# An RWKV attention layer with a 32-expert MoE on one core: z moved to ScalarE, its norm weights to the experts' split, one scan for the counts, and a new order of the rounds and seams

## The chip, the cores and the metric

One core of a Trainium2 chip. The time is the device time of one execution in microseconds. The kernel before has a median of 1735.44 us over 3 runs (1730.95 to 1735.58).

## The reference

`x` is 8 sequences of 512 tokens with 512 channels. With `xn` the layer norm of `x`, the output is `x + attention(xn) + ffn(xn)`:

```python
# attention (xx = previous token - token)
k, v, r, g = (xn + xx * tm_i) @ W_i.T        # four projections
wkv = scan over tokens: out = (a + e^u e^k v) / (b + e^u e^k); a = w a + e^k v; b = w b + e^k
o = (sigmoid(r) * wkv * sigmoid(g)) @ Wo.T ; attention = layernorm(o) * ln_g + ln_b
# ffn
z = w_norm * rmsnorm(xn)
probs = softmax(z @ w_router) ; 4 of 32 experts per token, at most 256 tokens per expert
out = sum of the 4 experts' (silu(z @ w_gate) * (z @ w_up)) @ w_down * prob
out += sigmoid(z @ w_shared_gate) * ((silu(z @ sw_gate) * (z @ sw_up)) @ sw_down)
```

Matrix products have fp32 accuracy: each operand is split into a rounded high part and the rest (`_hi`, `_lo`), and three products replace one.

## The kernel before

Everything is on one core, in three stages, each with hand-written orders of work for five queues (`sync`, `gpsimd`, `scalar`, `vector`, `tensor`). Engines meet only at semaphores; within a queue the order in the code is the order of execution, so an instruction that waits holds all that is queued behind it.

**Projection stage** (lines 115 to 1019): 8 rounds, one for each sequence. `first_round`, `one_round(1)`, a loop of two rounds, `one_round(6, tail=True)` and `last_round`. A round b holds: layer-norm statistics (`norm_stats`, `norm_scales`), `make_xn`, transposes on TensorE (`turn_xn`), the mixes for K, V, R and G (`make_mix` L681 on VectorE; `mix_hi` L455 on ScalarE; `mix_lo` L358 on GpSimd), the four projections (`project`, L957, each in two halves of 24 matmuls), exponentials, sigmoids and gates (`exp_k`, `gate_r` L470, `gate_g`, `make_ekv`, `make_gate` L702). For the FFN: z by token (`make_z` L629, VectorE), stored to HBM rows, and z transposed (`make_zT`, L650 and L657), from which `score` has the router's logits. `choose` (L705) finds the top 4, one-hot rows, and the running count `seen` (four additions, L733); `count` on TensorE turns the counts into positions; `assign` (L738 to L767) makes slots and weights; `scatter` (L372) writes token numbers into a table in HBM, 16 indirect DMAs a round issued by GpSimd, among the `mix_lo` of R and K.

**First seam**: in `last_round` the first experts' weights are loaded and split. After all scatters the table is read (`read_table`), indices are made, GpSimd gathers expert 0's rows of z, TensorE turns them.

**Expert stage** (L1021 to L1346): 32 experts of 256 slots. Per expert TensorE makes gate and up products for three chunks of the hidden units (`up_gate`, L1305), turns the next expert's rows (L1297), then the down product (L1332, 18 matmuls, chunk by chunk; each chunk waits for its `hidden_lo`). ScalarE's `rows_hi` (L1165) and VectorE's `rows_lo` (L1244) split the turned rows while the down product runs, and stand ahead of chunk 2's `hidden_hi` and `hidden_lo` (L1255).

**Output stage** (L1349 on): 8 batches, with 11 pieces of the shared expert each: `gate_up(f)` (L1930), `down(f)` (L1944), the output projection (L1961). Batch 0 also splits the shared weights piece by piece (`weight_hi`, `weight_lo`, `gate_lo`), `piece` holding one of each kind. VectorE's `fill(f)` puts the wkv recurrence (`sums` L1762 and L1764, `current`, `inverse`, `make_att`) and the sum over experts (`add_expert`) between the hidden products. **The second seam** is the last expert (`during_last`) and batch 0.

## Time and profile before

| | us |
|---|---|
| median of 3 runs | 1735.44 |
| the profiled execution | 1735.99 |
| its span | 1734.2 |
| projection rounds and first seam, to the first expert product | 468.0 |
| experts, to the first shared product | 435.0 |
| output stage | 831.2 |

TensorE is the busiest engine (1653.1 us), then VectorE (1275.4), GpSimd (885.7) and ScalarE (661.5). In the views, DVE is VectorE, ACT ScalarE, POOL GpSimd, PE TensorE's matmuls and PEld its weight loads. A timeline row has its start, its duration, the instruction, and in brackets how long its engine had stood still and what ended that.

### The profile page before, as it was taken

Reading aid. Unit: us, or ns where it says so; the run is one execution under the profiler, and the core shown is the slowest. Engines: PE = TensorE matmul, PEld = TensorE weight load, DVE = VectorE, ACT = ScalarE, POOL = GpSimd, SP = SyncE. Lnnn points to the kernel's source line nnn. Section 1 sums busy time; section 2 is a strip of 40 time slices with the busy share of each in tenths; the row PEclk is TensorE's granted clock in tenths of the full one; section 3 lists DMA queues with packets and bytes.
Section 4 is the critical chain, followed back from the end, with each engine's and each line's share of the span. In section 5 each row is a group of like instructions: output and inputs, shape, how many; then the busy total and the mean of one; then the engine's idle time right before and its main releaser. Section 6 shows DMA issues by size and latency. Waiting matters only on the chain.

```text
span 1734.2 us, 26081 instructions
## 1 busy us (share of the span) xinstructions
PE 1653.1 (95%) x8496; PEld 1402.8 (81%) x8496; DVE 1275.4 (74%) x1836; ACT 661.5 (38%) x1093; POOL 885.7 (51%) x733
## 2 busy tenths in 40 slices
PE   5889999998899999999998899999999999999998
PEld 4667777876699999999996688888788888888887
DVE  6999989998455555555559887786787768687776
ACT  4545545453466665666653312121121212112121
POOL 3778878886644444444436645252443524253351
PEclk9999999999999999999999999999999999999999
DMA  4354332433476666666687655465444344433431
GB/s 159 146 194 147 132 136 99 168 146 147 153 256 222 230 241 245 241 228 222 239 273 225 212 204 182 144 203 173 146 155 162 113 144 142 135 121 110 164 104 43
DMA packets 123087, 299.47 MB, mean 173 GB/s; under 512 B 20524, under 2 KB 31788, under 8 KB 118384
## 3 DMA queue, kind: packets, MB, share of 16 engines
q1 hardware_dynamic: 103248, 264.08, 42.9%
q0 software_dynamic: 19456, 33.67, 6.9%
q8 instruction: 50, 0.82, 0.2%
q10 hardware_dynamic: 288, 0.52, 0.1%
q14 instruction: 45, 0.37, 0.1%
HBM read 233.61 MB, written 81.36 MB: 182 GB/s over the span
## 4 chain that ended last, share of the span: by engine, by line
PE 69%; DVE 14%; issue 8%; POOL 4%; DMA 3%; ACT 2%; DVEq 0%; SPq 0%; POOLq 0%; ACTq 0%
PE bank L1930 24%; PE bank L1305 16%; PE bank L1944 12%; PE bank L1332 8%; PE bank L1961 5%; DVE mixf L681 3%; POOL slot_tokens L372 2%; PE bank L1297 2%; PE bank L957 2%; DMA z_rows<-z 1%; POOL mix L358 1%; DVE bank L650 1%; DVE z L629 1%; DVE s_wg L1834 1%; DVE ekv L697 1%
## 5 line engine op out<-in xcount | busy, mean ns | idle before, releaser
L957 PE MATMUL bank<-mix,w 128*128 128x512 f32 x1536 | 369.4, 398 | 27.5 <-DVE sr L702 11.0
L957 PEld LDWEIGHTS bank<-mix,w 128*128 128x128 f32 x1536 | 289.3, 191 | 97.9 <-DVE sr L702 10.6
L1930 PE MATMUL bank<-s_zT,s_wu 128*128 128x512 f32 x1056 | 256.3, 392 | 13.5 <-DVE s_act_g L1739 11.5
L1930 PE MATMUL bank<-s_zT,s_wg 128*128 128x512 f32 x1056 | 254.2, 389 | 0.7 <-ACT s_act_g L1650 0.5
L1944 PE MATMUL bank<-s_wd,s_h 128*128 128x512 f32 x1056 | 253.9, 389 | 0.9 <-DVE s_h L1745 0.9
L1930 PEld LDWEIGHTS bank<-s_zT,s_wu 128*128 128x128 f32 x1056 | 198.7, 189 | 57.9 <-issue 16.8
L1930 PEld LDWEIGHTS bank<-s_zT,s_wg 128*128 128x128 f32 x1056 | 197.9, 188 | 43.1 <-issue 1.5
L1944 PEld LDWEIGHTS bank<-s_wd,s_h 128*128 128x128 f32 x1056 | 198.1, 188 | 42.6 <-issue 1.3
L1126 POOL TENSOR_TENSOR e_wg<-e_g_in,e_wg 128x1408 fp32r<-128x1408 f32 x31 | 100.3, 3236 | 210.4 <-ACT e_wg L1150 210.4
L1562 POOL DMA_INDIRECT s_picked<-y_rows,s_slot x128 | 140.5, 1098 | 84.9 <-DVE s_total L1795 45.2
L358 POOL TENSOR_TENSOR mix<-mixf,mix 128x512 fp32r<-128x512 f32 x116 | 154.8, 1353 | 51.5 <-ACT mix L455 50.5
L1661 ACT ACTIVATE s_h<-s_act_g 128x512 fp32r<-128x512 f32 x88 | 55.6, 632 | 295.6 <-DVE s_act_g L1739 293.8
L372 POOL DMA_INDIRECT slot_tokens<-token,slot x128 | 140.8, 1100 | 47.5 <-issue 35.0
L1650 ACT ACTIVATE s_act_g<-bank 128x512 f32<-128x512 f32 x88 | 52.4, 596 | 280.8 <-PE bank L1930 274.2
L1305 PE MATMUL bank<-e_xT,e_wg 128*128 128x256 f32 (+1 forms) x1152 | 152.2, 282 | 0.0
L1305 PE MATMUL bank<-e_xT,e_wu 128*128 128x256 f32 (+1 forms) x1152 | 152.1, 282 | 0.0
L1305 PEld LDWEIGHTS bank<-e_xT,e_wg 128*128 128x128 f32 (+1 forms) x1152 | 144.3, 180 | 3.0 <-DVE e_xT L1244 0.4
L1305 PEld LDWEIGHTS bank<-e_xT,e_wu 128*128 128x128 f32 (+1 forms) x1152 | 142.1, 180 | 0.0
L1332 PE MATMUL bank<-e_wd,e_h 128*128 128x512 f32 (+1 forms) x576 | 140.1, 396 | 0.0
L1795 DVE SCALAR_TENSOR_TENSOR s_total<-s_picked,s_rec,s_total 128x512 f32<-128x512 f32 x128 | 130.2, 1017 | 3.7 <-DVE s_total L1795 0.5
L455 ACT ACTIVATE mix<-mixf 128x512 fp32r<-128x512 f32 x128 | 78.7, 630 | 131.5 <-DVE mixf L681 115.9
L1582 POOL TENSOR_TENSOR s_att<-s_gate,s_att 128x512 fp32r<-128x512 f32 x32 | 47.3, 1478 | 155.3 <-ACT s_att L1676 155.3
(158 smaller groups left out, 2451.9 us busy)
## 6 DMA issues: line engine op xcount, KB each, us to landing
s_wu<-wu_split SPq DMA_DIRECT2D x77, 512.0 KB
e_g_in<-in_w_gate SPq DMA_DIRECT2D x32, 704.0 KB
e_u_in<-in_w_up SPq DMA_DIRECT2D x32, 704.0 KB
e_d_in<-in_w_down SPq DMA_DIRECT2D x32, 512.0 KB
y_rows<-e_y SPq DMA_DIRECT2D x32, 512.0 KB, 2.9
s_zT<-zT_parts SPq DMA_DIRECT2D x16, 1024.0 KB, 7.0
zT_parts<-zT_hi SPq DMA_DIRECT2D x8, 1024.0 KB
zT_parts<-zT_lo SPq DMA_DIRECT2D x8, 1024.0 KB
```

Of the source, the lines that this page charges most:

```text
L358: pool.tensor_tensor(mix[:, i % 2, k, 1, :], mixf[:, k, :], mix[:, i % 2, k, 0, :].bitcast(F32), ALU.subtract).then_inc(lo_made, 1)
L372: pool.indirect_dma_start(d["slots"], bass.IndirectOffsetOnAxis(ap=slot[:, at:at + 1], axis=0), token[:, at // TOPK:at // TOPK + 1], None, ...
L455: act.activation(mix[:, i % 2, k, 0, :], mixf[:, k, :], ACT.Copy).then_inc(hi_made, 1)
L957: last = pe.matmul(pj[m][:], w[i][:, w_part, k, m * P:(m + 1) * P], mix[:, i % 2, k, x_part, :], start=(k == 0 and q == 0), stop=(k == KC ...
L1126: pool.tensor_tensor(wg[half][:, 1, :], g_in[half][:], wg[half][:, 0, :].bitcast(F32), ALU.subtract).then_inc(wg_lo, 1)
L1305: last = pe.matmul(gu[f][0:m, which, :], w[half][:, w_part, k * F + f0:k * F + f0 + m], xT[half][:, x_part, k, :], start=(q == 0 and k == ...
L1332: last = pe.matmul(yp[c][:], h[0:m, f, h_part, c * P:(c + 1) * P], wd[half][0:m, w_part, f, :], start=(f == 0 and q == 0), stop=(f == NF - ...
L1562: pool.indirect_dma_start(picked[:, k, :], None, d["y_flat"], bass.IndirectOffsetOnAxis(ap=slot[:, j * TOPK + k:j * TOPK + k + 1], axis=0) ...
L1795: dve.scalar_tensor_tensor(total[:, j, :], picked[:, k, :], rec[:, at:at + 1], total[:, j, :], ALU.mult, ALU.add).then_inc(picked_used, 1)
L1930: last = pe.matmul(into[:], w[:, w_part, k, :], zT[:, x_part, k, :], start=(q == 0 and k == 0), stop=(q == 2 and k == KC - 1))
L1944: last = pe.matmul(yp[j][:], h[:, i, h_part, j * P:(j + 1) * P], wd[f][:, w_part, :], start=(f == 0 and q == 0), stop=(f == NFS - 1 and q ...
L1961: last = pe.matmul(ob[j % 2][:], att[m][:, x_part, j * P:(j + 1) * P], wo[m][:, w_part, :], start=(m == 0 and q == 0), stop=(m == KC - 1 a ...
```

## The change

What it does:

- `make_z` goes to ScalarE, as xn times its rms factor, without the norm weights; z gets four buffers. The weights come in when an expert's turned rows are split: `rows_hi` and `rows_lo` work on four pieces of 256 columns with a per-partition factor. The copies of scales, slots and weights into `keep` are ScalarE's as well (`keep_route`).
- The four additions of `seen` become one `tensor_tensor_scan` over 32 x 5 columns.
- The low part of the V mix is made by VectorE, not GpSimd. The scatters of a round are spread among the low parts of R, G and K (`MORE` is 6), 4 alone at a round's start; slots and tokens have two buffers.
- `count` comes between R's halves, `assign` after G's mixes; the first gates of a round stand within `make_zT`; assign(0) moves into round 1.
- A new order for the last round: `score(LAST)` is its first product, `choose` and `assign` follow V's mixes, R's and G's low parts are VectorE's; first weights wait for V's first half, second weights' up and down parts for the gather.
- At the second seam gate pieces 1 to 4 have a buffer of their own and are split in the last expert, at four places of each queue, with the first scans, the first reciprocal and the four bases. Hidden products of the shared expert (all but the last piece) are written to PSUM.

```diff
+        def one_round(b, half, uses, second=False, tail=False):
+            last = NT * TOPK
+            if second:
+                pool.wait_ge(table_zeroed, 16)
+            at = 0 if second else MORE
+            scatter(b - 1, 1 - half, at, at + KC)
             norm_scales(b + 1, 1 - half)
-            mix_lo_among(b, R_, b - 1, MORE)
-            scatter(b - 1, MORE + KC, NT * TOPK)
-            mix_lo(b, G_)
-            scatter(b, 0, SOME)
-            mix_lo_among(b + 1, K_, b, SOME)
-            scatter(b, SOME + KC, MORE)
+            mix_lo_among(b, R_, b - 1, 1 - half, at + KC, last)
+            if second:
+                scatter(b - 1, 1 - half, at + 2 * KC, last - KC)
+                at = last - 3 * KC
+            mix_lo_among(b, G_, b - 1, 1 - half, at + 2 * KC, last)
+            scatter(b, half, 0, MORE - KC)
+            mix_lo_among(b + 1, K_, b, half, MORE - KC, MORE)
+            if tail:
+                scatter(b, half, MORE, last)
...
+        def make_z(b, half):
+
+            act.wait_ge(pow_step, (b + 1) * POWS)
+            for j in range(NT):
+                act.wait_ge(xn_made, b * NT + j + 1)
+                wait(act, z_stored[j], b * 16)
+                act.activation(z[:, j, :], xn[:, j, :], ACT.Copy, scale=r2[:, half, j:j + 1]).then_inc(z_made, 1)
+            act.activation(keep["rec"][:, bass.ds(b * REC, 2 * NT)], scales[:, half, :], ACT.Copy).then_inc(scales_kept, 1)
+
+        def keep_route(b, half):
+            act.wait_ge(rec_made, b + 1)
+            act.activation(keep["slot"][:, bass.ds(b * NT * TOPK, NT * TOPK)], slot[:, half, :], ACT.Copy)
+            act.activation(keep["rec"][:, bass.ds(b * REC + 2 * NT, REC - 2 * NT)], rec[:],
+                           ACT.Copy).then_inc(route_kept, 1)
...
+            if second:
+                keep_route(0, 0)
+            make_z(b + 1, 1 - half)
+            keep_route(b, half)
             gate_r(b, 0)
...
-                route.step(dve.tensor_reduce(chosen[:], oh[:].rearrange("p (j k) e -> p j e k", j=NT), AX.X, ALU.add))
+                route.link(dve.tensor_reduce(counted[:, :, 1:NT + 1], oh[:].rearrange("p (j k) e -> p e j k", j=NT),
+                                             AX.X, ALU.add))
+                dve.tensor_tensor_scan(seen[:].rearrange("p e j -> p (e j)"), fresh[:].rearrange("p e j -> p (e j)"),
+                                       counted[:].rearrange("p e j -> p (e j)"), 0.0, ALU.mult,
+                                       ALU.add).then_inc(chosen_made, 1)
             dve.tensor_scalar(token_id, token_id, float(T), None, ALU.add)
-            route.link(dve.tensor_copy(seen[:, 0, :], seen[:, NT, :]))
-            for j in range(NT):
-                ins = dve.tensor_tensor(seen[:, j + 1, :], seen[:, j, :], chosen[:, j, :], ALU.add)
-                if j < NT - 1:
-                    route.link(ins)
-            ins.then_inc(chosen_made, 1)
...
+        def one_round(b, half, uses, second=False, tail=False):
+            gates(b - 1, 2)
+            if second:
+                assign(0, 0, 0)
             for k in range(KC):
                 make_mix(b, half, V_, k)
+            for k in range(KC):
+                mix_lo(b, V_, k)
             norm_stats(b + 1)
-            if second:
-                for j in range(NT):
-                    make_z(1, 1, j)
             for k in range(KC):
                 make_mix(b, half, R_, k)
             choose(b)
-            make_z(b + 1, 1 - half, 0)
-            make_z(b + 1, 1 - half, 1)
-            make_ekv(b, 0)
-            make_ekv(b, 1)
-            make_z(b + 1, 1 - half, 2)
-            make_z(b + 1, 1 - half, 3)
-            keep_scales(b + 1, 1 - half)
-            make_mix(b, half, G_, 0)
-            make_mix(b, half, G_, 1)
-            make_ekv(b, 2)
-            make_ekv(b, 3)
-            make_mix(b, half, G_, 2)
-            make_mix(b, half, G_, 3)
-            assign(b)
+            for m in range(KC):
+                make_ekv(b, m)
+            for k in range(KC):
+                make_mix(b, half, G_, k)
+            assign(b, half, uses)
             for k in range(KC):
                 shift_difference(b + 1, 1 - half, k)
-            if tail:
-                make_zT(LAST, FIRST_HALF)
             for k in range(KC):
                 make_mix(b + 1, 1 - half, K_, k)
-            if not tail:
-                make_zT(b + 1, 1 - half)
-            make_gate(b, 0)
-            make_gate(b, 1)
+            make_zT(b + 1, 1 - half, lambda: gates(b, 0))
...
         def last_round():
+            gates(LAST - 1, 2)
+            for k in range(KC):
+                make_mix(LAST, FIRST_HALF, V_, k)
             choose(LAST)
+            for k in range(KC):
+                mix_lo(LAST, V_, k)
+            assign(LAST, FIRST_HALF, B // 2 - 1)
+            for k in range(KC):
+                make_mix(LAST, FIRST_HALF, R_, k)
+            for k in range(KC):
+                mix_lo(LAST, R_, k)
+            for m in range(KC):
+                make_ekv(LAST, m)
             for k in range(KC):
                 make_mix(LAST, FIRST_HALF, G_, k)
             for k in range(KC):
                 mix_lo(LAST, G_, k)
             first_weights()
+            gates(LAST, 0)
...
-            count(b)
             turn_xn(b + 1, 2)
             turn_xn(b + 1, 3)
             turn_r2(b + 1, 1 - half)
             project(b, R_, 0)
+            count(b)
             project(b, R_, 1)
             project(b, G_, 0)
-            if tail:
-                score(LAST)
-            project(b, G_, 1, {3: lambda: turn_score(LAST)} if tail else {})
+            project(b, G_, 1)
 
         def last_round():
-            project(LAST, K_, 0)
-            project(LAST, K_, 1, {1: lambda: count(LAST)})
+            score(LAST)
+            project(LAST, K_, 0, {2: lambda: turn_score(LAST)})
+            project(LAST, K_, 1, {3: lambda: count(LAST)})
...
+            sp.wait_ge(shared["v_done"], B * KC - 2)
             load(0, 0)
 
         def second_weights():
             sp.wait_ge(shared["r_done"], B * KC)
-            load(1, 1)
+            load(1, 1, lambda part: sp.wait_ge(gathered[0], 32))
 
         def read_table():
-            sp.wait_ge(shared["scattered"], 16 * B * NT * TOPK)
+            for half in range(2):
+                sp.wait_ge(shared["scattered"][half], 16 * (B // 2) * NT * TOPK)
             sp.dma_start(table[:], d["table"]).then_inc(table_loaded, 16)
...
         def rows_hi(e, half):
             act.wait_ge(turned, e + 1)
-            for i in range(2):
-                act.activation(xT[half][:, 0, 2 * i:2 * i + 2, :],
-                               xt[i][:].rearrange("p (k s) -> p k s", k=2), ACT.Copy).then_inc(x_hi, 1)
+            for k in range(KC):
+                turned_k = xt[k // 2][:, (k % 2) * CAP:(k % 2 + 1) * CAP]
+                act.activation(xT[half][:, 0, k, :], turned_k, ACT.Copy, scale=norm_col[:, k:k + 1]).then_inc(x_hi, 1)
...
         def rows_lo(e, half):
-            for i in range(2):
-                dve.wait_ge(x_hi, e * 2 + i + 1)
-                dve.tensor_tensor(xT[half][:, 1, 2 * i:2 * i + 2, :], xt[i][:].rearrange("p (k s) -> p k s", k=2),
-                                  xT[half][:, 0, 2 * i:2 * i + 2, :].bitcast(F32), ALU.subtract).then_inc(x_lo, 1)
+            for k in range(KC):
+                dve.wait_ge(x_hi, e * KC + k // 2 * 2 + 2)
+                turned_k = xt[k // 2][:, (k % 2) * CAP:(k % 2 + 1) * CAP]
+                dve.scalar_tensor_tensor(xT[half][:, 1, k, :], turned_k, norm_col[:, k:k + 1],
+                                         xT[half][:, 0, k, :].bitcast(F32), ALU.mult, ALU.subtract).then_inc(x_lo, 1)
...
+    def hidden_at(f, i):
+
+        return ob[f % 2][:] if f < NFS - 1 else act_g[:, i, :]
...
             weight_lo(D, 1)
+            weight_lo(D, 2)
+            pool.wait_ge(piece_lo[G], AHEAD + 1)
             pool.memset(picked[:], 0.0).then_inc(setup, 1)
+            pool.wait_ge(c_loaded, 32)
+            for j in range(NT):
...
+        def last_second():
+            weight_hi(G, 1)
+            weight_hi(G, 2)
+            weight_hi(G, 3)
+
+        def last_third():
+            weight_hi(G, 4)
+
+        def last_fourth():
+            weight_hi(U, 1)
+            weight_hi(D, 1)
+            for j in range(NT):
+                make_base(0, j)
...
             hidden_lo(e, 1)
             hidden(e, 2)
             if more:
                 rows_lo(e + 1, 1 - half)
+            else:
+                output_early[2]()
             hidden_lo(e, 2)
             if more:
                 down_lo(e + 1, 1 - half)
+            else:
+                output_early[3]()
 
...
+        def last_third():
+            gate_lo(2)
             dve.wait_ge(setup, 3)
             sums(0, 0, 0)
-            hidden(0, 0, 0)
-            rounds(dve, one_round)
-
-        return lambda: gate_lo(0), main
+
+        def last_fourth():
+            gate_lo(3)
+            gate_lo(4)
+            current(0, 0)
+            inverse(0, 0)
```

## Rows read from the trace of the kernel before

**Rows 1.** The page's first part: busy time, share of the span, instructions
```profile
PE 1653.1 (95%) x8496; PEld 1402.8 (81%) x8496; DVE 1275.4 (74%) x1836; ACT 661.5 (38%) x1093; POOL 885.7 (51%) x733
```

**Rows 2.** Busy time by stage: span, busy us (instructions) by engine, granted clock, DMA share, GB/s
```profile
79.00:141.92 62.92, 51.58 (x228) 41.10 (x227) 59.52 (x109) 30.28 (x53) 51.34 (x47) 0.95 0.36 134
...
352.37:468.04 115.67, 101.07 (x440) 80.92 (x440) 86.69 (x173) 49.38 (x80) 79.55 (x74) 0.94 0.40 148
468.00:904.00 436.00, 435.99 (x3134) 411.69 (x3134) 239.57 (x383) 269.26 (x448) 196.80 (x96) 1.00 0.67 239
903.04:1007.33 104.29, 91.56 (x386) 72.46 (x385) 92.00 (x76) 37.49 (x66) 63.99 (x49) 0.98 0.69 216
1020.93:1107.97 87.04, 87.04 (x385) 72.10 (x385) 67.42 (x69) 18.89 (x30) 36.42 (x28) 1.00 0.54 174
```

**Rows 3.** TensorE's timeline, 340 to 355 us: start, us, instruction [idle before, releaser]
```profile
343.88 6.07 PE L957 MATMUL bank<-mix,w 128*128 128x512 f32 x24 [0.25 <-ACT sr L470]
352.37 5.71 PE L957 MATMUL bank<-mix,w 128*128 128x512 f32 x24 [2.42 <-DVE sr L702]
```

**Rows 4.** Busy time, one steady projection round
```profile
300.42:352.37 51.95, 49.24 (x226) 39.57 (x227) 48.33 (x93) 26.33 (x47) 43.70 (x41) 1.00 0.38 142
```

**Rows 5.** VectorE's groups by form, 0 to 460 us: count, busy us, mean ns, idle before
```profile
L681 DVE SCALAR_TENSOR_TENSOR mixf<-xx,keep_const,xnT 128x512 f32<-128x512 f32 x128 | 124.2, 1024 | 2.7 <-POOL mix L358 2.5
L629 DVE SCALAR_TENSOR_TENSOR z<-xn,r,norm_w 128x512 f32<-128x512 f32 x32 | 35.7, 1149 | 10.3 <-DMA z_rows<-z 8.2 <-issue 1.6
L650 DVE SCALAR_TENSOR_TENSOR bank<-xnT,keep_const,bank 128x512 f32<-128x512 f32 x32 | 23.3, 750 | 0.6
```

**Rows 6.** Timeline of VectorE and GpSimd, 250 to 260 us
```profile
252.84 4.64 DVE L681 SCALAR_TENSOR_TENSOR mixf<-xx,keep_const,xnT 128x512 f32<-128x512 f32 x1
...
253.12 3.80 POOL L358 TENSOR_TENSOR mix<-mixf,mix 128x512 fp32r<-128x512 f32 x3
```

**Rows 7.** VectorE's timeline, `assign` of round 1
```profile
124.67 0.67 DVE L745 TENSOR_TENSOR oh<-oh,bank 128x512 f32<-128x512 f32 x1
...
128.74 0.21 DVE L764 TENSOR_TENSOR rec<-rec,valid 128x16 f32<-128x16 f32 x1
```

**Rows 8.** Timeline of one expert, 700 to 715 us
```profile
709.38 1.09 ACT L1165 ACTIVATE e_xT<-bank 128x512 fp32r<-128x512 f32 x2 [0.50 <-PE bank L1297]
710.01 1.29 DVE L1244 TENSOR_TENSOR e_xT<-bank,e_xT 128x512 fp32r<-128x512 f32 x2 [0.68 <-ACT e_xT L1165]
...
711.22 0.41 DVE L1255 TENSOR_TENSOR e_h<-e_act_g,e_h 96x256 fp32r<-96x256 f32 x1
711.71 0.19 PEld L1332 LDWEIGHTS bank<-e_wd,e_h 96*128 96x128 f32 x1
```

**Rows 9.** Line 1762, one of the two scans: duration ns min/median/max
```profile
L1762 DVE TENSOR_TENSOR_SCAN s_b_sum<-keep_decay,s_ek x32: 1211/1220/2326, 905.0 to 1690.5; 128x512 f32<-128x512 f32 x32
```

**Rows 10.** ScalarE's groups by form, 0 to 460 us
```profile
L455 ACT ACTIVATE mix<-mixf 128x512 fp32r<-128x512 f32 x128 | 78.7, 630 | 131.5 <-DVE mixf L681 115.9 <-issue 14.4
L428 ACT ACTIVATE xn<-x_in,scales 128x512 f32<-128x512 f32 x32 | 24.3, 806 | 37.8 <-POOL var_eps L348 21.5 <-POOL scales L347 12.5 <-DVE z L629 3.8
...
L470 ACT ACT_TABLE_LOAD x8 | 10.3, 1283 | 0.4 <-issue 0.3
```

**Rows 11.** TensorE's timeline, round 0: the first G product
```profile
67.58 11.48 PE L957 MATMUL bank<-mix,w 128*128 128x512 f32 x48 [1.42 <-issue]
```

**Rows 12.** Timeline, the first seam
```profile
426.31 0.16 DVE L755 TENSOR_TENSOR slot<-s,s 128x16 uint32<-128x16 f32 x1
...
434.23 0.98 POOL L372 DMA_INDIRECT slot_tokens<-token,slot  x1 [5.94 <-issue]
...
454.22 0.97 POOL L372 DMA_INDIRECT slot_tokens<-token,slot  x1 [0.30 <-issue]
...
464.05 1.98 PE L1297 MATMUL bank<-keep_const,e_rows 128*128 128x128 f32 x8 [8.16 <-DMA e_rows<-z_rows,keep_index]
```

**Rows 13.** TensorE's weight loads, the last expert's down product
```profile
898.78 3.99 PEld L1332 LDWEIGHTS bank<-e_wd,e_h 128*128 128x128 f32 x18
```

More of the change, by code:

```diff
@@ L365, in weight_lo, with scatter @@
                                    ALU.subtract).then_inc(w_lo[i], 1)
-        def scatter(b, first, last):
+        def scatter(b, half, first, last):
             if first == 0:
@@ L1074, in sync, with load @@
     def sync(sp):
-        def load(e, half):
+        def load(e, half, paced=lambda part: None):
             wait(sp, wg_lo, e - 1)
@@ L1197, in one_expert @@
             silu(e, 1)
+            if not more:
+                output_early[1]()
             hidden_hi(e, 1)
@@ L1267, in one_expert @@
             hidden(e, 1)
+            if not more:
+                output_early[1]()
             hidden_lo(e, 1)
```

333 lines of the change are left out of this document (160 added, 173 removed).

## The prediction

> **What bounds the kernel now.** The page's first part says TensorE is busy 95% of the span [rows 1], which leaves at most some 80 us, so the question is only where TensorE stands still. I read the busy table by stage next [rows 2]. From 468 to 904 us (experts), and in the shared expert's second batch, TensorE has no gap: there nothing can be won, only lost. The gaps are in the first 468 us (eight projection rounds), and in the first shared-expert batch, whose way from its first product to its first output projection takes 104.29 us, where the same way in the next batch takes 87.04. So at most 17.2 us lie there.
>
> Then the projection round. Four steady rounds lie between 141.92 and 352.37 [rows 2, 3], 52.6 us each; in the last of them (51.95) VectorE is busy 48.33 [rows 4]. There TensorE waits 2.42 for VectorE's gate product, 0.25 for ScalarE's sigmoid, and 24 matmuls that otherwise take 5.5 take 6.07 [rows 3]: without these a round is **48.6 us**, TensorE's floor. VectorE sets the rest, and not by its arithmetic alone: L650, which reads and writes PSUM, has a mean of 0.750 us, L681, the same operation on SBUF alone, 1.024 over 128 of them, so 35 us in all are waiting inside this one form [rows 5]. z (L629), of the same form, has a mean of 1.149. The timeline shows why: one L681 takes 4.64 and ends only after three GpSimd subtractions in a row have ended [rows 6].
> The Trainium skill, "SBUF — State Buffer", section "SBUF: two separate sides", calls this an exclusive lock: a VectorE instruction with two SBUF inputs against a GpSimd one that reads SBUF, the loser blocked entirely. The trace agrees, with 4.64 against 0.750.
>
> **Part 1, the steady projection round.** Off VectorE go: four z (4 x 1.15 = 4.6, and waits for z's stores), the copies of scales, slots and weights (about 0.8), four count additions and a copy (bounds 0.9, at 0.17 to 0.21 as `assign`'s short steps [rows 7], and 2.1 if they are stretched too; 1.6 taken), and the one long wait of [rows 6], since no four subtractions in a row are left on GpSimd (about 3.9). On it come: four V subtractions (0.69 each as L1244 [rows 8], 2.8), one scan of 160 columns (bounds 0.4 and 0.8, by 512 columns at 1.2 or 2.3 [rows 9]; I take 0.6) and a copy (0.17). Net 10.9 - 3.6, about -7: VectorE falls from 48.3 to some 41, under the floor. GpSimd loses 4 x 1.35 and keeps 16 scatters; ScalarE takes z at 4 x 0.8 as L428 [rows 10] and the copies, 26.3 of 52 us [rows 4] become 30. z and the copies there are hidden behind matmuls as long as ScalarE is ahead of its sigmoids.
> That is the catch. The position count moves from after V to between the halves of R, and ScalarE's copy of the route (it waits for the end of `assign`) is queued ahead of gate_r(b,0). Counted from the end of R's first half: count 0.15, `assign` from L745 to L764 4.28 with one stretched step [rows 7] and one copy more, 4.4; two short copies 0.45 (as two or three of `assign`'s short steps); the table load 1.28 [rows 10] and a sigmoid of 0.6: 6.9 us. TensorE comes to G after 5.5 and needs it: it waits 1.4 (bounds 0.5 if nothing in `assign` is stretched, 3 if two steps are). So a round is 48.6 + 1.4 = 50.0, and the wait for VectorE's gates goes, since gates(b,0) now stand ahead of most of make_zT. Rounds 2 to 5: 4 x (52.6 - 50.0) = **-10.4**.
>
> **Part 2, the first rounds.** In round 0 G starts at 67.58 after a wait of 1.42 [rows 11]. Without z, choose(0) starts some 5 us earlier; G then starts with the end of R's second half and the transposes, at 65.4, 2.2 sooner, and the count (0.3) is later: **-2.5**. ScalarE's z(0), 2.9 us, delays the G weights, but GpSimd is busy until later. Round 1 takes 62.92 with TensorE busy 51.58 [rows 2]: 11.3 of waits, for the count (late by the stretched additions) and for K, where GpSimd's scatters stand between the subtractions. The count moves to a place where it isn't late, the scatters go out of K. But assign(0) comes in (4.2 on VectorE), norm_scales follow 2 to 3 us later, and transposes wait 0.7: 48.6 + 1.4 + 0.7 = 50.7 (the granted clock of 0.95 in that row taken as full again without the waits), **-12.2**.
>
> **Part 3, the last two rounds and the first seam**, 115.67 us [rows 2]. Now: the slots of the last round are ready at 426.3, then 16 scatters run to 455.2, of which 5.94 is one hold of the queue; the gather lands at 464.05 after TensorE stood 8.16 [rows 12], and the first expert product is at 468.04. After: round 6 is 50.0, score(LAST) waits 0.8 for zT. From its start: slots at 15 (logits 4.8, choose 5.2, V subtractions 2.6, half of assign 2.4); GpSimd has by then put out round 6's ten scatters (10 x 1.27 = 12.7; one is 0.97 + 0.30 [rows 12]). Sixteen are 20.3, and from the last one to the landed gather 8.9 pass as now: 44.2 without a hold, 50.1 with one. TensorE is there at 44.5. I take half, 3, and 4.2 from turn to product as now: 50.0 + 0.8 + 44.5 + 3 + 4.2 = 102.5, **-13.2** (bounds -16 and -8; the weight loads now start after V's first half and so fall among these scatters, as they do now around the hold). Sum of parts 1 to 3: **-38** (bounds -44 and -22).
>
> **Part 4, the experts, where I expect a loss.** The norm weight goes into the split of the turned rows: 2 ScalarE copies of 512 columns become 4 of 256 with a pointer scale, 2 VectorE subtractions become 4 scalar_tensor_tensor. Behind them on VectorE stands the subtraction for the third hidden chunk, which TensorE's down product needs at its weight load of 711.71. Today it ends at 711.22 + 0.41 = 711.63 [rows 8]: 0.08 us of cover. Now: two ScalarE copies take 1.09, so one per 0.49; 256 columns 0.30 to 0.35 each. A pointer scale and bias cost 0.17 in duration and 0.05 in spacing (L428 0.806 against L455 0.630 [rows 10]). Two of 256 are there at about 710.1 to 710.3 instead of 710.01. VectorE: two subtractions take 1.29, one per 0.60; a scalar_tensor_tensor takes 0.06 more than such a subtraction for 512 (L650 0.750 [rows 5] against 0.69), so 0.39 for 256: 4 x 0.39 = 1.56 against 1.20. Late by 0.12 to 0.30 + 0.36, less the cover: 0.4 to 0.6 per expert. I take 0.5: 31 x 0.5 = **+15.5** (bounds: +6 if only the extra starts count, +39 by the rival below). The down product has no other slack, as TensorE is never idle here.
> The Trainium skill, "ScalarE: Activation LUTs", section "Rules for kernel authors", budgets about 0.3 us per ACTIVATE with a pointer bias and 0.83 ns per element. By it, as an estimate, four of 256 are 2.05 us against 1.45 for two of 512, and if they don't overlap the third chunk is 1.0 late: +31 us in place of +15.5. The two copies of [rows 8] take 1.09 where the budget has 1.45, so I stay with the sum.
>
> **Part 5, the second seam**, 17.2 us at most. Gate pieces 1 to 4, the first scans, the bases and one reciprocal move into the last expert, and the hidden product goes to PSUM, which takes VectorE's waits for the port away from its subtractions. But in the last expert both scans stand ahead of the third chunk's subtraction: gate_lo 0.7 and two scans of 1.2 to 2.3 each [rows 9], 3.1 to 5.3 in all. The third chunk is made at 899.94; with these and its own subtraction of 0.4 it is split at 903.4 to 905.6. The down product starts its loads at 898.78 [rows 13] and wants it after 12 of them, 2.6 later, at 901.4: 2.0 to 4.2 lost, 3.5 taken, since GpSimd is busy beside. GpSimd then has in a row the wait for D2 (silu(0) + 0.6), its 1.3, the memset 1.8, four base additions 5.2 and four gathers 5.2 (each as a scatter, 1.27) ahead of U2's split: TensorE waits some 2.4. With 2.5 left of today's waits (12.7 by the busy table [rows 2]): 8.4 of 17.2 remain, **-9** (bounds -13 and -2). The other seven batches: all changes are off TensorE's path and VectorE has slack; 0, bounds -1 and +2.
>
> **Sum.** Span 1734.2; 1734.2 - 38 + 15.5 - 9 = 1702.7. The profiled run reports 1735.99, 1.8 above its span, and the median is 1735.44: **1704 us**.
>
> **Rivals.** (a) The third chunk isn't late: were ScalarE's pieces and VectorE's to overlap better than the spacings, the cover holds. For it: ScalarE's copies from PSUM overlap already (1.09 for two of 0.6). Against: 0.08 us of cover. 1704 - 15 = 1689. (b) The route copy blocks more: `assign` is stretched in two or three steps beside alternating scatters and subtractions, and the sigmoids and K's copies behind it are late as well; 2.5 us more in seven rounds, 1721. For it: its waits in [rows 7]; against: it has one such step today. (c) The scaled copies don't overlap at all: 0.41 + 0.17 = 0.58 each, the fourth at 711.70, the third chunk at 712.92, 1.25 late, 39 us for 15.5: 1728. The skill's budget, in the sentence above, lies between this and the forecast. (d) **Slower**: each scaled copy holds ScalarE as long as L428 does for 512 columns, 0.80: four take 3.2 in place of 1.0, the third chunk is 2.1 late, 65 us in the experts: 1754. It decides from 47 / 31 = 1.5 us per expert on. Against it: half the columns. (e) VectorE isn't relieved in the rounds because its waits move to other instructions: rounds stay at 52.6 and parts 2 and 3 bring half, 1727.
>
> **How the numbers follow.** Forecast 0.47, (a) 0.17, (b) 0.16, (c) 0.09, (d) 0.04, (e) 0.07. The forecast's own range is 1694 to 1714; with (a), (b) and most of (c) the range is 1685 to 1727, which leaves out 2 in 10. About 0.3% (5 us) is what a measurement of this kernel can tell from no change. Faster by more: all but (d) and the high ends of (c) and (e): 0.92; same 0.03; slower 0.05.
>
> **What would show it.** In the profile after: rounds at 50 us with a wait of the G product for ScalarE's sigmoid, none for VectorE's gates; no L681 over 2 us in V; VectorE near 41 per round; first expert product at 430. An expert period of 14.1 instead of 13.62 with a TensorE wait in the down product; no wait there means (a), over 15 means (d). In the second seam one wait of 3 to 4 us in the last expert's down product and one for U2's split. Wrong would be: a new hold of a queue in the last round, or z on ScalarE late for xn.

## The result, and the profile after

The changed kernel takes 1738.14 us (median of 9 runs), the kernel before 1734.13 us beside it: a ratio of 1.0027, 95% interval 1.0016 to 1.0039. The prediction was 1704 us, with 1685 to 1727 as its range. The profiled execution has a span of 1736.3 us, against 1734.2.

The sum hides two shifts that cancel. In the table each stage ends where TensorE starts the next one's first product.

| stage | before | after | difference | predicted |
|---|---|---|---|---|
| start to the first expert product | 468.04 | 454.99 | -13.0 | -38 |
| experts, to the first output product | 435.0 | 451.76 | +16.8 | +19 (15.5 and 3.5) |
| first output batch, to its first attention product | 104.3 | 101.2 | -3.1 | -12.5 |
| the rest | | | +1.5 | 0 |

The page of the kernel after, first part (compare [rows 1]), and its busy table (columns as in [rows 2]; the rows are the first output batch, the next one, one steady projection round, and the stretch of [rows 4]):

```profile
PE 1662.9 (96%) x8496; PEld 1405.3 (81%) x8496; DVE 1243.6 (72%) x1848; ACT 693.3 (40%) x1213; POOL 848.5 (49%) x707
```
```profile
906.75:1007.91 101.16, 90.60 (x385) 72.66 (x384) 82.03 (x72) 32.88 (x58) 62.52 (x48) 0.98 0.65 209
1021.51:1108.55 87.04, 87.04 (x385) 72.07 (x384) 67.56 (x69) 18.53 (x30) 36.39 (x28) 1.00 0.54 173
281.06:334.25 53.19, 50.37 (x226) 40.94 (x227) 41.33 (x87) 29.13 (x53) 37.05 (x36) 0.96 0.38 138
300.42:352.37 51.95, 49.13 (x223) 40.23 (x222) 40.46 (x86) 28.14 (x52) 38.03 (x36) 0.97 0.37 135
```

VectorE's busy time in a round fell from 48.3 us to 41.3, as predicted, ScalarE's went to 29 and GpSimd's to 37. No engine beside TensorE is near the round's length, and the round still takes 53.0 us (mean of rounds 2 to 5) against 52.6. TensorE's timeline, every wait for the first product of G (start, us, instruction, idle before and releaser):

```profile
122.08 18.21 PE L934 MATMUL bank<-mix,w 128*128 128x512 f32 x72 [4.19 <-ACT sr L486]
176.05 18.19 PE L934 MATMUL bank<-mix,w 128*128 128x512 f32 x72 [3.60 <-ACT sr L486]
229.25 16.60 PE L934 MATMUL bank<-mix,w 128*128 128x512 f32 x72 [2.82 <-ACT sr L486]
281.06 18.18 PE L934 MATMUL bank<-mix,w 128*128 128x512 f32 x72 [3.03 <-ACT sr L486]
334.25 17.93 PE L934 MATMUL bank<-mix,w 128*128 128x512 f32 x72 [2.82 <-ACT sr L486]
387.14 12.77 PE L934 MATMUL bank<-mix,w 128*128 128x512 f32 x48 [2.77 <-ACT sr L486]
438.18 11.40 PE L934 MATMUL bank<-mix,w 128*128 128x512 f32 x42 [2.70 <-ACT sr L486]
```

The wait for VectorE's gates (2.42 in [rows 3]) has turned into a wait for ScalarE's sigmoid: the place that the prediction named, at twice its size or more. A second cost follows some of these waits, and not all. 72 matmuls take 18.2 us at 122.08, 176.05 and 281.06 and 17.9 at 334.25; at full clock they take 16.6 (72 x 0.23), and so they do at 229.25. The granted clock is 0.62 of full speed from 334.3 to 338.0, right after the wait, so most of that stretch runs at the lower of its two levels, 1.2 GHz; from 229.25 to 233.0, after a wait of the same 2.82 us, it is 1.00.

What ScalarE waited for stands on VectorE and GpSimd, in the round of 334.25:

```profile
326.06 0.69 DVE L748 TENSOR_TENSOR oh<-oh,bank 128x512 f32<-128x512 f32 x1 [2.86 <-PE bank L912]
326.78 2.43 DVE L750 COPY counted<-seen 128x32 bf16<-128x32 bf16 x1
329.09 0.67 DVE L751 TENSOR_REDUCE pos<-oh 128x16 f32<-128x512 f32 x1
...
331.53 0.22 DVE L769 TENSOR_TENSOR rec<-rec,valid 128x16 f32<-128x16 f32 x1
```
```profile
326.57 2.56 POOL L354 TENSOR_TENSOR mix<-mixf,mix 128x512 fp32r<-128x512 f32 x2
```
```profile
331.87 0.22 ACT L450 ACTIVATE keep_slot<-slot 128x16 uint32 x1 [5.46 <-DVE rec L769]
332.00 0.20 ACT L451 ACTIVATE keep_rec<-rec 128x20 f32 x1
332.22 1.28 ACT L486 ACT_TABLE_LOAD   x1
333.51 1.09 ACT L486 ACTIVATE sr<-bank 128x512 f32<-128x512 f32 x2
```

R's first half has been done since 325.5, yet ScalarE is idle for 5.46 us, because its copy of the route stands ahead of the sigmoids and waits for VectorE's last step. A copy of 32 columns takes 2.43 us in that chain, next to two GpSimd subtractions in a row; alone, in the last round, it takes 0.21. Of the rounds with a longer wait, the one of 176.05 has this copy at 3.00. The one of 122.08 has it at 0.27, and there two later steps of 16 columns are the long ones:

```profile
114.87 2.01 DVE L760 TENSOR_TENSOR slot<-s,s 128x16 uint32<-128x16 f32 x1
...
117.42 1.92 DVE L766 TENSOR_TENSOR rec<-ex,rtot 128x16 f32<-128x16 f32 x1
```

In the experts the third chunk's subtraction ends later than in [rows 8], and TensorE waits a little in every down product (TensorE and VectorE, expert at 700 us):

```profile
707.54 1.67 PE L1327 MATMUL bank<-e_wd,e_h 96*128 96x512 f32 x6 [0.20 <-DVE e_h L1244]
```
```profile
705.50 1.66 DVE L1233 SCALAR_TENSOR_TENSOR e_xT<-bank,keep_const,e_xT 128x256 fp32r<-128x256 f32 x4 [0.92 <-ACT e_xT L1148]
707.08 0.41 DVE L1244 TENSOR_TENSOR e_h<-e_act_g,e_h 96x256 fp32r<-96x256 f32 x1
```

The expert period is 14.11 us instead of 13.62. The row shows 0.20 us of waiting, but the wait costs more: the 18 products of the down projection take 4.70 us from their start to the next gate product, and 4.22 in the run below where the wait is gone.

### The profile page after: what moved, and what is told of

It is laid out like the page before. It is cut to its first block, busy times and chain, and to the rows that moved or that the text cites. A ratio compares the mean times of both kernels' runs of the same rounds, so it can differ in the third digit from the quotient of the medians.

```text
span 1736.3 us, 26220 instructions
## 1 busy us (share of the span) xinstructions
PE 1662.9 (96%) x8496; PEld 1405.3 (81%) x8496; DVE 1243.6 (72%) x1848; ACT 693.3 (40%) x1213; POOL 848.5 (49%) x707
## 4 chain that ended last, share of the span: by engine, by line
PE 75%; DVE 11%; issue 5%; ACT 3%; POOL 3%; DMA 2%; DVEq 0%; ACTq 0%; SPq 0%; another core or an unknown queue 0%; POOLq 0%
PE bank L1986 23%; PE bank L1300 15%; PE bank L934 13%; PE bank L2000 12%; PE bank L2017 5%; PE bank L1327 3%; DVE e_xT L1233 2%; PE bank L1292 2%; ACT e_xT L1148 2%; POOL slot_tokens L368 1%; PE bank L876 1%; PE bank L893 1%; DVE mixf L686 1%; DVE e_h L1244 1%; DVE s_total L1838 1%
## 5 line engine op out<-in xcount | busy, mean ns | idle before, releaser
L934 PE MATMUL bank<-mix,w 128*128 128x512 f32 x1536 | 375.3, 403 | 26.9 <-ACT sr L486 21.9
L934 PEld LDWEIGHTS bank<-mix,w 128*128 128x128 f32 x1536 | 295.6, 195 | 93.9 <-issue 26.0
L1108 POOL TENSOR_TENSOR e_wg<-e_g_in,e_wg 128x1408 fp32r<-128x1408 f32 x31 | 101.2, 3263 | 223.4 <-ACT e_wg L1132 223.4
L1327 PE MATMUL bank<-e_wd,e_h 128*128 128x512 f32 (+1 forms) x576 | 149.1, 403 | 7.7 <-DVE e_h L1244 7.7
L1686 ACT ACTIVATE s_h<-bank 128x512 fp32r<-128x512 f32 x80 | 47.8, 598 | 265.7 <-DVE bank L1782 265.7
L354 POOL TENSOR_TENSOR mix<-mixf,mix 128x512 fp32r<-128x512 f32 x88 | 120.4, 1378 | 47.0 <-ACT mix L471 45.9
L1838 DVE SCALAR_TENSOR_TENSOR s_total<-s_picked,s_rec,s_total 128x512 f32<-128x512 f32 x128 | 138.3, 1080 | 3.7 <-DVE s_total L1838 0.5
L1327 PEld LDWEIGHTS bank<-e_wd,e_h 128*128 128x128 f32 (+1 forms) x576 | 103.6, 189 | 40.7 <-DVE e_h L1244 21.2
```

The lines of the kernel that those rows point to most:

```text
L354: pool.tensor_tensor(mix[:, i % 2, k, 1, :], mixf[:, k, :], mix[:, i % 2, k, 0, :].bitcast(F32), ALU.subtract).then_inc(lo_made, 1)
L934: last = pe.matmul(pj[m][:], w[i][:, w_part, k, m * P:(m + 1) * P], mix[:, i % 2, k, x_part, :], start=(k == 0 and q == 0), stop=(k == KC ...
L1108: pool.tensor_tensor(wg[half][:, 1, :], g_in[half][:], wg[half][:, 0, :].bitcast(F32), ALU.subtract).then_inc(wg_lo, 1)
L1327: last = pe.matmul(yp[c][:], h[0:m, f, h_part, c * P:(c + 1) * P], wd[half][0:m, w_part, f, :], start=(f == 0 and q == 0), stop=(f == NF - ...
L1838: dve.scalar_tensor_tensor(total[:, j, :], picked[:, k, :], rec[:, at:at + 1], total[:, j, :], ALU.mult, ALU.add).then_inc(picked_used, 1)
```

## The experiments

Each run is compared with the kernel before on the same chip. To compare it with the changed kernel I divide its ratio by 1.0027 and take 1738 us as 1. The ratios given in the expectations of the first four runs were meant against the changed kernel.

| run | median us | ratio to before, 95% | against the changed kernel |
|---|---|---|---|
| e1_route_late | 1722.7 | 0.9939 (0.9923 to 0.9956) | -15 |
| e2_copy_late | 1729.4 | 0.9975 (0.9965 to 0.9984) | -9 |
| e3_chunk_first | 1722.6 | 0.9938 (0.9919 to 0.9957) | -15 |
| e4_no_weights | 1721.2 | 0.9936 (0.9919 to 0.9954) | -16 |
| e5_second_seam | 1737.6 | 1.0030 (1.0018 to 1.0042) | +1 |
| e6_all | 1706.3 | 0.9840 (0.9824 to 0.9857) | -32 |
| e7_v_on_gpsimd | 1744.5 | 1.0068 (1.0051 to 1.0085) | +7 |
| e9_gate_first | 1706.8 | 0.9843 (0.9825 to 0.9861) | -32 |
| e10_z_on_vector | 1725.2 | 0.9954 (0.9936 to 0.9971) | -13 |
| e11_no_seam | 1706.9 | 0.9837 (0.9821 to 0.9854) | -33 |

**The route copies behind the sigmoids.**

```diff
@@ scalar, one_round
-            keep_route(b, half)
             gate_r(b, 0)
 ...
             gate_r(b, 3)
+            keep_route(b, half)
@@ scalar, last_round
+            for m in range(KC):
+                gate_r(LAST, m)
             first_gate_up()
             keep_route(LAST, FIRST_HALF)
-            for m in range(KC):
-                gate_r(LAST, m)
```

> In every projection round after the first, ScalarE's copies of the route (keep_route of the round's own batch) go behind the four sigmoids of R (behind gate_r(b, 3)), and in the last round the four sigmoids also go ahead of the first expert's weight copies; nothing else changes. Theory A (the 3 us wait of TensorE for the first sigmoid of R is the wait of ScalarE for VectorE's route, and the slow restart of TensorE after it is part of its price): the wait for sr in rounds 1 to 6, 21.9 us in 7, falls under 4 us, the 18.2 us of the following 72 matmuls fall back to 16.6, rounds go from 53.0 to 49 to 50 us, the first expert product moves from 454.99 to about 432, and the kernel is 20 to 25 us faster (ratio 0.986 to 0.989). Theory B (the sum of VectorE's work and the contention with GpSimd fixes the round): the wait moves to another operand and rounds stay within 1 us of 53.0, ratio 0.996 to 1.002.

The wait for the sigmoid is gone from every round. Rounds 2 to 5 take 48.9 to 49.5 us, at a granted clock of 1.00. That is theory A, and 3.8 us a round for the position of two short copies, slow matmuls behind the wait included. VectorE's sum does not bound the round: it is busy 44.4 of 49.3 us here and nobody waits for it. The total came out smaller than expected (15 us, not 20 to 25; first expert product at 440.06, not 432), because the last round has a limit of its own. TensorE's timeline of this run:

```profile
382.29 1.14 PE L893 MATMUL bank<-zT_lo,wr 128*68 128x512 f32 x4 [2.48 <-DVE zT_lo L661]
...
435.46 1.98 PE L1292 MATMUL bank<-keep_const,e_rows 128*128 128x128 f32 x8 [6.12 <-DMA e_rows<-z_rows,keep_index]
```

score(LAST) starts 17.8 us sooner (382.29 against 400.07), but the 16 scatters on GpSimd follow the slots, most of them 1.27 us apart, and the gather now ends the wait: 6.12 us, where the changed kernel, being late, waited 1.56.

**The copy of the counts behind the route.**

```diff
@@ vector, assign
             dve.wait_ge(pos_read, b + 1)
-            dve.tensor_copy(counted[:, :, 0], seen[:, :, NT])
 ...
             dve.tensor_tensor(weight, weight, valid[:], ALU.mult).then_inc(rec_made, 1)
+            dve.tensor_copy(counted[:, :, 0], seen[:, :, NT])
```

> VectorE's copy of the counts into the scan's input (the 32 columns counted <- seen in assign), which took 2.43 us beside GpSimd's low parts, goes to the end of assign, behind the last step of the route; it can then stretch nothing that ScalarE waits for. Theory A (the stretched copy is what made the chain from R's first half to the route 8.75 us instead of the 6.9 predicted): the route is ready about 2 us earlier in rounds 1 to 5, TensorE's wait for the first sigmoid falls from about 2.9 to about 1 us, each round gets 2 to 3.5 us shorter (with the half-clock restart), the kernel 10 to 17 us faster (ratio 0.990 to 0.994). Theory B (it is the port that is held and not this copy: whichever small operation of VectorE comes next then waits in its place): the chain keeps its length and the kernel is within 3 us of the changed one (0.998 to 1.002).

Between the two theories. VectorE in the same round (compare L750 above):

```profile
322.31 0.69 DVE L748 TENSOR_TENSOR oh<-oh,bank 128x512 f32<-128x512 f32 x1 [2.86 <-PE bank L912]
323.03 0.69 DVE L750 TENSOR_REDUCE pos<-oh 128x16 f32<-128x512 f32 x1
323.75 1.67 DVE L751 TENSOR_SCALAR valid<-pos 128x16 f32<-128x16 f32 x1
...
326.97 0.22 DVE L768 TENSOR_TENSOR rec<-rec,valid 128x16 f32<-128x16 f32 x1
```

The reduction passes unhindered, and the next small step, a tensor_scalar of 16 columns, takes 1.67 instead of 0.17. The hold has moved, and 0.8 us of it is gone. The Trainium skill, "SBUF — State Buffer", section "SBUF: two separate sides", has copies and tensor_scalar in two-port modes fully blocked while a GpSimd instruction holds the shared pair; the trace agrees, with 2.43 for the copy and 1.67 for the tensor_scalar, each until GpSimd's second subtraction has ended.
In rounds 2 to 5 the waits for the sigmoid are 2.68, 2.01, 2.23 and 2.01 us; in the changed kernel they are 3.60, 2.82, 3.03 and 2.82. So 0.8 to 0.9 us is gone from each. Rounds 2 and 3 got shorter by just that (53.97 to 53.03 and 51.60 to 50.81 us). Rounds 4 and 5 gained 2.1 to 2.4 us (53.39 to 50.99 and 52.94 to 50.80), since TensorE also restarts at full clock:

```profile
278.91 16.59 PE L934 MATMUL bank<-mix,w 128*128 128x512 f32 x72 [2.23 <-ACT sr L486]
329.69 16.60 PE L934 MATMUL bank<-mix,w 128*128 128x512 f32 x72 [2.01 <-ACT sr L486]
```

Of the 6.3 us that four rounds gained, 3.3 are wait and 2.9 are clock. That the shorter wait brought the clock back is not shown: a wait of 2.82 us is followed by 16.60 in one round of the changed kernel and by 17.93 in another, and in two of the runs below, which leave the rounds as they are, by these (the first e3_chunk_first, the second e4_no_weights):

```profile
229.76 19.43 PE L934 MATMUL bank<-mix,w 128*128 128x512 f32 x72 [2.82 <-ACT sr L486]
335.36 16.59 PE L934 MATMUL bank<-mix,w 128*128 128x512 f32 x72 [2.82 <-ACT sr L486]
```

**The third chunk ahead of the next rows, and the rows without the weights.** The first moves hidden_hi(e, 2) ahead of rows_hi(e + 1) on ScalarE and hidden_lo(e, 2) ahead of rows_lo(e + 1) on VectorE:

```diff
             hidden(e, 2)
+            if not more:
+                output_early[2]()
+            hidden_lo(e, 2)
             if more:
                 rows_lo(e + 1, 1 - half)
-            else:
-                output_early[2]()
-            hidden_lo(e, 2)
```

> In the experts the two halves of the third hidden chunk (hidden_hi(e, 2) on ScalarE, hidden_lo(e, 2) on VectorE) go ahead of the copies and differences of the next expert's turned rows; the number of instructions is unchanged. Theory A (the experts' 0.49 us each are the third chunk standing behind four instructions instead of two): TensorE's wait for e_h in the down product disappears, the period falls from 14.11 to 13.62, minus 15 us (ratio 0.990 to 0.992). Theory B (the longer rows' work itself is the price): the wait moves to the next expert's rows or to the down product's weights, of which down_lo now ends later, and the period stays above 14.0 (ratio 0.998 to 1.002).

> The norm weights are left out of the experts: the turned rows are copied and subtracted in two instructions of 512 columns on each engine, as before the change, without the per-partition factors (this leaves the weights out of the experts' input). All else is the changed kernel. Theory A (the four scaled copies and four scaled differences in the place of two and two cost the experts' 0.49 us): the period falls from 14.11 to 13.6, minus 15 to 16 us (ratio 0.990 to 0.992). Theory B (the period was lengthened by something else of the change, such as the early loads of the output stage): it stays at 14.1 (ratio 0.999 to 1.001).

The stage of the experts took 451.76 us in the changed kernel, 437.1 in the first run and 436.4 in the second. Theory A in both: the four scaled pieces are the cause, and the price is the third chunk's place behind them, not their work. In the reordered run all pieces are there, TensorE's wait in the down product is gone (but for 1.34 us in the last expert, whose order is unchanged), and nothing else is late:

```profile
701.54 4.38 PE L1327 MATMUL bank<-e_wd,e_h 128*128 128x512 f32 x18
```

(In the first run's profile the stage ahead, which it doesn't touch, took 5 us longer than in the changed kernel's, at a granted clock of 0.95 instead of 0.97; the medians show the experts' 15 us.)

**The second seam.** GpSimd's weight_lo(U, 2) goes ahead of the first gathers, and VectorE's sums(0, 0, 0) from ahead of hidden_lo(e, 2) to behind it.

> Two moves in the seam from the experts to the output stage, the rest is the changed kernel: GpSimd splits the shared expert's up piece 2 (weight_lo(U, 2)) ahead of the first four gathers instead of behind them, and VectorE's first two scans of the last expert (sums(0, 0, 0)) go behind the subtraction of the third hidden chunk. Theory A (the order on GpSimd and on VectorE is the price in this seam): TensorE's wait of 3.55 us for s_wu at 926.79 and the slow 12 matmuls behind it (4.61 instead of 2.9) go, 5 us, and the wait of 1.35 us in the last down product goes; from the first product of the output stage to the first attention product the time falls from 101.2 to 96 us, the kernel is 5 to 7 us faster than the changed one. Theory B (VectorE's sum of work in the first batch, whose waits of 0.6 to 1.8 us in seven chunks follow later, sets this stage): what is gained at the front comes back as longer waits for VectorE's hidden products, and the stage stays above 99 us, gain 1 to 3 us.

Both waits went and nothing was gained: theory B, though not for its reason. The stage of the experts is 2.0 us shorter, the first output batch 4.2 longer (105.4). TensorE in that batch:

```profile
920.18 4.41 PE L1987 MATMUL bank<-s_zT,s_wg 128*128 128x512 f32 x12 [2.94 <-ACT s_act_g L1676]
...
932.72 4.58 PE L1987 MATMUL bank<-s_zT,s_wg 128*128 128x512 f32 x12 [2.70 <-ACT s_act_g L1676]
```

ScalarE was itself waiting, for a piece of weights and then for VectorE's attention product, in the same run:

```profile
918.16 0.63 ACT L1726 ACTIVATE s_wg<-s_piece 128x512 fp32r<-128x512 f32 x1 [5.75 <-DMA s_piece<-in_sw_gate]
...
931.46 0.63 ACT L1705 ACTIVATE s_att<-s_gate 128x512 fp32r<-128x512 f32 x1 [5.67 <-DVE s_gate L1829]
```

SP issues that piece behind the load of down piece 2, which waits for GpSimd to split piece 1. Both waits end at about the same moment of the kernel as in the changed one (its two copies start at 916.95 and 930.53), though the batch began 3.4 us sooner. So the start of the batch moved, and what it waits for did not.

**All moves together**, with one more: VectorE's two index copies go between gate_lo(0, 0) and up_lo(0, 0) in first_weights.

> All the moves together: the route copies behind the sigmoids in the rounds and the last round, VectorE's copy of the counts behind the route, the third hidden chunk ahead of the next rows, the two moves of the second seam, and in the last round VectorE's two index copies between the differences of the first gate and up weights instead of behind both (GpSimd's first gather waited 1.6 us longer for them in the run with the route copies moved). If the gains add: 15.4 + 15.6 + 5 to 7 + 1.5 us below the changed kernel's 1738, so 1698 to 1701, the ratio to the kernel before 0.979 to 0.981, with rounds of 49.2 us, an expert period of 13.6 and the first expert product at 438. If they share a cause or VectorE becomes the bound of the rounds, less than 30 us come out, 1708 or more.

32 us below the changed kernel and 28 below the kernel before: the best of all kernels here, with two others equal to it. The moves of rounds and experts add (rounds of 49.0, experts 435.6 us, first expert product at 437.90). What misses the 1698 to 1701 is the first output batch, 104.8 us. GpSimd's split of U1 next to VectorE's moved scans:

```profile
872.63 4.57 POOL L1620 TENSOR_TENSOR s_wu<-s_piece,s_wu 128x512 fp32r<-128x512 f32 x1 [4.40 <-ACT s_wu L1726]
```

In the changed kernel it takes 2.79. The second seam's run, the only other one with the scans moved, has 4.29 there, and a batch of 105.4 us.

**The scans back, the first gated product ahead of the gathers.**

> The run with all moves, but with VectorE's scans of the last expert left where the change has them (ahead of the third chunk's subtraction), and with GpSimd's first gated product (gated_sum(0, 0)) also ahead of the first gathers. In the run with all moves the stage from the first product of the output stage to the first attention product took 104.8 us, against 101.2 in the changed kernel, although TensorE's waits for U2 and for the third chunk were gone. Theory A (the late scans ran beside GpSimd's split of U1, which took 4.57 us instead of about 2.2, so the load of down piece 2 and, behind it on SP's queue, every later piece came 2 us late, and ScalarE's sigmoid products stood behind VectorE's first attention product, which waits for GpSimd behind the gathers): the stage falls to 96 to 99 us, the kernel to 1698 to 1702, ratio to the kernel before 0.979 to 0.982, with the 1.35 us wait of the last down product back. Theory B (the pieces' DMAs themselves are late in this seam, whatever the order): the stage stays at 101 us or more, 1703 to 1707.

The numbers are those of theory B: the batch takes 101.9 us. The split of U1 takes 2.30 us again and 2.9 us of the 104.8 are gone, but not the 6 to 9 of theory A. The split of down piece 3 stands behind the gathers, as it does in the changed kernel, and with it the load of piece 4. ScalarE in this run:

```profile
902.91 0.63 ACT L1727 ACTIVATE s_wd<-s_piece 128x512 fp32r<-128x512 f32 x1 [7.48 <-DMA s_piece<-in_sw_down]
```

**Without the two seam moves.**

> The run with all moves, without the two moves in the seam to the output stage (U2's split stays behind the gathers, the scans ahead of the third chunk's subtraction): route copies late, copy of the counts late, third chunk first, index copies between. The two seam moves together gained nothing by themselves (1737.6 against 1738.1 us of the changed kernel). Theory A (moves in different stages add): the stage from the first output product to the first attention product is back at 101 us and the kernel at 1703 to 1707, that is within 3 us of the run with all moves (1706.3). Theory B (an earlier start of the output stage makes its piece loads later against TensorE, so the seam takes back part of what the rounds and experts give): more than 1708.

Theory A: 100.7 us for the batch, and the same total within the intervals. In the profiles of the other runs that leave this seam as the change has it, the batch takes 100.9 to 102.4 us (101.2 in the changed kernel), so 100.7 and 101.9 can't be told apart. Outside that scatter lie only the two kernels with the scans moved, 104.8 and 105.4. Moving U2's split together with the gated product is worth nothing that these runs can show; U2's split without the scans' move was not run alone.

**Two parts of the change undone**, each in the kernel with the route copies late.

> The run with the route copies moved (rounds of 49.2 us) with one part of the change undone: the low parts of V's mixes in rounds 1 to 6 are made by GpSimd again, as in the kernel before, and not by VectorE. Theory A (moving them bought something, since GpSimd with its scatters was the later engine): TensorE waits for mix_lo of V or R behind GpSimd's scatters, rounds grow to 50 to 52 us, the kernel is 5 to 15 us slower than that run (ratio to the kernel before 0.997 to 1.002). Theory B (TensorE hides either): rounds stay within 0.3 us of 49.2 and the ratio stays at 0.994; then this part of the change bought nothing by itself.

> The run with the route copies moved (rounds of 49.2 us), with another part of the change undone: from round 1 on VectorE makes z again (four products of 512 columns by the row scale, without the norm weights, which stay with the experts), between its route and its products of V, and ScalarE only copies the scales. Theory A (taking z from VectorE was needed): VectorE's 41 us per round become 44 to 45, and with the waits for V, R and the route TensorE waits again: rounds of 50 to 52 us, 5 to 15 us slower than that run (ratio to the kernel before 0.997 to 1.003). Theory B (VectorE had room for it): rounds stay within 0.4 us of 49.2, ratio 0.993 to 0.995.

V's low parts back on GpSimd cost 22 us: rounds 2 to 5 go from 49.2 to 52.3 us in the mean, with waits in three of them each for xn (1.6 to 1.7, behind GpSimd's scales) and for the sigmoid (1.4 to 1.6). Theory A, beyond its range. z back on VectorE gives rounds of 49.5, 49.2, 52.0 and 49.2 us (50.0 in the mean; the long one has waits of 0.80 for xn and 1.82 for the sigmoid), VectorE is busy 47.8 of 50 us, and the kernel takes 1725.2 against 1722.7 us. The intervals overlap, so of z no more is shown than that it is worth little once V and the route are settled.

## Why the prediction was wrong

Point by point, in its own steps.

**The floor of a round and VectorE's relief (part 1): right.** 48.6 us was predicted for a round without waits (51.95 less its three terms is 48.7), and the run with the route copies late has 48.9 to 49.5. VectorE went to 41.3, 41 predicted. Rival (e) is out as a mechanism, though rounds did stay at 53: VectorE was relieved, and another wait took the place.

**The wait for gate_r (part 1): the step that failed.** The place, the releaser and the queue position were right, the size was not. The chain from the end of R's first half to TensorE's restart takes 8.75 us (325.50 to 334.25) and was put at 6.9. `assign` takes 5.69 instead of 4.4, because its copy of 32 columns is held for 2.43, and 0.5 passes before it starts. This is rival (b) in kind, with one held step in rounds 2 to 5 and two in round 1. The waits of rounds 2 to 5 are therefore 3.60, 2.82, 3.03 and 2.82, 3.1 in the mean, instead of 1.4.

The sum then put at nothing what such a wait can cost behind it. In three of the four rounds the next 72 matmuls took 1.3 to 1.6 us more than at full clock, 1.1 a round in the mean. So the 3.0 us between the predicted 50.0 and the 53.0 measured are 1.7 of wait, 1.1 of clock and 0.2 of floor: 12 us in rounds 2 to 5, of which 6.7 are wait and 4.5 clock. The rows that would have warned are in the kernel before, where one of two like waits is followed by slow matmuls (granted clock 0.77 from 193.62 to 201, and 1.00 from 246.72 to 252.5):

```profile
193.62 7.34 PE L957 MATMUL bank<-mix,w 128*128 128x512 f32 x24 [2.34 <-DVE sr L702]
246.72 5.77 PE L957 MATMUL bank<-mix,w 128*128 128x512 f32 x24 [2.32 <-DVE sr L702]
```

The 6.07 of [rows 3], which the prediction took away as 0.57 too long, is not such a case: it stands ahead of the wait of 2.42, at a granted clock of 1.00.

**The first rounds (part 2): half right.** K of round 1 starts at 75.9 as predicted (76.5), but round 1 then waits 2.34 for the score and 4.19 for the sigmoid, each with 1.5 to 1.6 us of half clock behind it, and takes 58.7 us from score to score for 50.7 forecast.

**The last rounds and the first seam (part 3): too good.** No long hold came (2.27 behind the first scatter, 5.94 before), where the sum took half of one. But the last round has the same fault as the others: keep_route(LAST) stands behind the first expert's weight copies and ahead of the sigmoids, another 2.70. The run without it shows what was mis-sized beside: the score waits 2.48 for zT (0.8 forecast) and the gather 6.12 (3 forecast), 4.8 us of the 10 between the predicted 430 and its 440.06; GpSimd's subtractions in round 1, five waits of 0.5 to 1.1 between its scatters, are 4.4 more. The gather is late because each term of its chain was too small: the first scatter starts 19.8 us after the score (15 for the slots in the sum), the sixteen take 22.9 (20.3), and 10.5 pass from the last to the turn of the gathered rows (8.9).

**The experts (part 4): right.** 0.49 us each against 0.5 predicted, with the mechanism shown by two runs. Of the two parts of the term, ScalarE's four pieces take 1.57, for 1.2 to 1.4 by the 0.30 to 0.35 each of the sum, and VectorE's four 1.66, predicted 1.56. The Trainium skill, "ScalarE: Activation LUTs", section "Rules for kernel authors", would give an estimated 2.05 for ScalarE's four; the trace has 1.57. Rivals (a), (c) and (d) are out. (In (c), 712.92 is 1.21 us behind 711.71, not 1.25, which makes 1726 of its 1728.) The wait in the last down product was 1.35, not 3.5, as the scans were not stretched (1.2 each).

**The second seam (part 5): mis-sized.** U2's split is late as predicted (3.55 against 2.4), with half clock behind it (4.61 us for 12 matmuls that take 2.9, granted clock 0.60), and 7.0 us of waits for VectorE's hidden products are left where 2.5 were forecast. The batch gained 3.1 us where 12.5 were in the sum. In the experiments, taking the wait for U2 away left the batch no shorter; what sets the 14 us above the next batch's 87.04 stays open.

The signs: of the forecast's 34 us of error, 12 are the route wait and its clock in four rounds, 13 the other rounds and the first seam, 9 the second seam; the experts came out 2 us better and the later batches 1.5 worse. The chance of 0.92 for faster rested on parts 1 to 3, whose bounds (-44 to -22) did not hold -13. Both ends were worked out at full clock, while TensorE's busy time for the same matmuls up to the first expert product is 408.7 us, as it was before (407.7), and 403.5 in the run with the route copies late.

## What to carry to other kernels

A short copy that nobody needs soon is dangerous on an in-order queue when it waits for the end of another engine's chain: cost each instruction queued behind it, not the copy. A wait that a change creates costs its length and, sometimes, slow matmuls after it. Read both off all the waits of that length that the trace already has, and put the second into the bounds: here it came after some and not after others. When work is inserted ahead of something that has only 0.08 us of cover, try the order the other way round first: here the order gave back all of the 15 us.

## What was not expected of the hardware

- The length of a wait of TensorE doesn't tell what follows it. After 2.82 us the next 72 matmuls took 16.6, 17.9 and 19.4 us in different rounds and runs. After 2.0 to 2.2 they took 16.6 in rounds 3 to 5 of the run with the copy late, but after 2.13 in its round 1 the granted clock was 0.61 for 4 us. What decides is not shown.
- The smallest instructions are held as long as large ones: L750, 32 columns of bf16, takes 0.213 at its shortest, 2.428 in the median and 2.995 at its longest over the eight rounds (the view gives ns).

```profile
L750 DVE COPY counted<-seen x8: 213/2428/2995, 82.3 to 415.0; 128x32 bf16<-128x32 bf16 x8
```

- The hold works the other way too: GpSimd's split of one 128x512 piece took 1.3 us undisturbed and 4.57 beside VectorE's scans and subtractions.
